# Layer four of a gated attention and mixture-of-experts network: two half blocks of the shared expert side by side, and one batch's routed results added by GpSimd

## What is computed

```python
# x: (4, 256, 256), normed row by row before it comes in; I_SH = 704, E = 8 experts, top 2, I_MOE = 176
probs = softmax(x @ W_router.T);  rw, sel = top_k(probs, 2)
g, u = split(x @ Ws_gate_up, 704)                    # shared expert, every token
sh = (silu(g) * u) @ Ws_down
shared_out = sh * sigmoid(x @ W_sgate.T)
gu = einsum('th,ehi->eti', x, We_gate_up)            # routed experts, two a token
eo = einsum('eti,eih->eth', silu(gu[..., :176]) * gu[..., 176:], We_down)
x_out = x + tanh(g_ffn[3]) * (shared_out + weighted sum of the token's two eo)
```

## Time and profile before

| | |
|---|---|
| median of 3 runs | 852.88 us (851.64, 852.88, 859.55) |
| profiled execution, its own time | 859.66 us |
| its span, first to last instruction | 857.9 us |
| busy: PE, DVE, ACT, POOL | 715.5, 546.8, 348.9, 206.9 us |
| mean granted TensorE clock | 0.908 |
| stage of the shared expert on PE | about 714 to 775 us |
| 23 routed tiles on PE | about 777 to 837 us |
| end: shared down 2 and 3, results back, stores | 837 to 858 us |

### The profile page before, as it was taken

The page is one execution under the profiler, slowest core; times in us unless marked ns, Lnnn a source line. Parts: engine busy times, 40 slices in busy tenths (PEclk is TensorE's granted clock), DMA queues, the critical chain, the costliest instruction groups (busy, mean ns, idle before and its releaser), DMA issues. The chain is left out here.

```text
span 857.9 us, 13857 instructions
## 1 busy us (share of the span) xinstructions
PE 715.5 (83%) x4399; PEld 473.9 (55%) x4399; DVE 546.8 (64%) x1655; ACT 348.9 (41%) x617; POOL 206.9 (24%) x299
## 2 busy tenths in 40 slices
PE   9999987878877745968786998976888889998995
PEld 4543556656764632646665776743233226776774
DVE  6787888886755965577675453445876856513554
ACT  2653555555437611512013413425468784212220
POOL 0003782001000220011413451542233220251331
PEclk9999999998888966879998799998589999999998
DMA  6993420400000400000133050012000033032314
GB/s 201 337 204 96 140 87 8 140 11 2 3 1 1 148 1 0 1 1 1 54 116 118 32 185 26 22 53 70 1 2 3 1 124 82 26 111 61 104 66 166
DMA packets 55487, 60.17 MB, mean 70 GB/s; under 512 B 13832, under 2 KB 48729, under 8 KB 55417
## 3 DMA queue, kind: packets, MB, share of 16 engines
q1 hardware_dynamic: 50328, 45.96, 18.8%
q0 software_dynamic: 4848, 13.28, 4.4%
q10 hardware_dynamic: 240, 0.05, 0.0%
HBM read 34.86 MB, written 24.20 MB: 69 GB/s over the span
## 5 line engine op out<-in xcount | busy, mean ns | idle before, releaser
L1856 ACT ACTIVATE arenas<-psum 128x512 f32<-128x512 f32 (+5 forms) x81 | 55.4, 703 | 59.7 <-PE psum L1095 40.5
L3053 DVE TENSOR_REDUCE arenas<-psum 128x2 f32<-128x512 f32 x96 | 62.1, 685 | 19.6 <-PE psum L1652 18.3
L1095 PE MATMUL psum<-conb,shared 128*128 128x128 bf16 (+2 forms) x512 | 41.7, 240 | 19.4 <-POOL shared L909 9.2
L907 POOL TENSOR_SCALAR arenas<-arenas,small 128x1024 f32<-128x1024 f32 x8 | 9.0, 1121 | 202.4 <-DVE small L2798 202.4
L1095 PEld LDWEIGHTS psum<-conb,shared 128*128 128x128 bf16 (+2 forms) x512 | 36.5, 126 | 27.6 <-issue 16.1
L921 POOL DMA_INDIRECT experts_l<-shared,small x30 | 29.2, 975 | 82.4 <-ACT shared L2148 70.5
L1543 PE MATMUL psum<-arenas,early 128*128 128x256 f32 (+1 forms) x192 | 43.9, 383 | 1.3 <-issue 1.0
L1856 ACT ACTIVATE late<-psum 128x512 f32<-128x512 f32 (+1 forms) x51 | 24.5, 504 | 48.2 <-PE psum L1095 48.1
L1095 PE MATMUL psum<-con,early 128*128 128x128 f32 (+1 forms) x188 | 32.5, 294 | 11.7 <-DVE early L2296 4.0
L2192 ACT ACTIVATE early<-psum 128x1024 f32<-128x1024 f32 x32 | 32.4, 1036 | 23.5 <-PE psum L1669 23.2
L3018 DVE TENSOR_TENSOR shared<-shared,psum 128x128 f32<-128x128 f32 x30 | 8.5, 286 | 51.3 <-PE psum L1605 29.2
(11 more groups left out here) (435 smaller groups left out, 1819.2 us busy)
## 6 DMA issues: line engine op xcount, KB each, us to landing
sorted_l<-late SPq DMA_DIRECT2D x3, 1920.0 KB, 17.8
early<-sorted_l SPq DMA_DIRECT2D x6, 645.0 KB, 5.8
early<-in_L_ffn_sw SPq DMA_DIRECT2D x3, 1024.0 KB, 9.0
late<-sorted_l SPq DMA_DIRECT2D x23, 129.0 KB, 2.0
sorted_l<-late SPq DMA_DIRECT2D x1, 2944.0 KB, 24.0
early<-in_L_ffn_We_gate_up SPq DMA_DIRECT2D x2, 1408.0 KB
early<-in_L_ffn_expert_w SPq DMA_DIRECT2D x2, 1024.0 KB, 6.9
early<-in_L_ffn_w SPq DMA_DIRECT2D x1, 2048.0 KB, 8.3
```

The source lines that it names most:

```text
L907: pool.tensor_scalar(ha[s][:, rows], ha[s][:, rows], c2[s][:, t:t + 1], ROUND, ALU.mult, ALU.add)
L1095: last = pe.transpose(v[0:parts, at:at + k], src, idn[0:k, 0:k])
L1856: act.activation(dst, view(v), ACT.Copy, scale=scale).then_inc(f.drained(i, key), 1)
L3053: dve.tensor_reduce(nm, q3d(f.slot(0, ("max", w, k)), 2, S), X, ALU.max, negate=True)\
```

## The change

It does two things in layer four's feed-forward.

First, the half blocks of a pair of batches (0 and 1, 2 and 3) share one bank. Batches 0 and 2 have five blocks. The sixth entry of batch 1 (and 3) holds 64 features of batch 0 in partitions 0 to 63 and the same 64 features of batch 1 in partitions 64 to 127; `blocks3(n)` gives the blocks of a batch. Gate and up of such an entry are eight matmuls with a weight of 64 columns each, in turn for the lower and the upper half. ACT and DVE treat the entry as a whole block. The down product takes the 64 features of its batch from the half where they lie, so the last 64 rows of Ws_down are loaded twice, once into each half (a fourth load under "l3s"). Since down 0 now needs the last entry of batch 1, and down 2 that of batch 3, their waits name it. Two of batch 2's blocks are put before down 0, and DVE's `add_shared(0, 0)` moves behind the second block of batch 2.

Second, POOL adds the routed results of batch 3 to x: four tensor_scalar with the weights, one tensor_tensor that sums the two experts, one tensor_tensor into x, then it signals x3_ready. DVE adds batches 0 to 2 as before, does `add_shared(1, 2)` ahead of them, and `add_shared(1, 3)` last, behind POOL's signal.

```diff
@@ plan of stage l3f
-             B=([0, 1, 2, 3], 1, [("sh", n, j) for n in range(B) for j in range(SC3)]))
+             B=([0, 1, 2, 3], 1, [("sh", n, j) for n in range(B) for j in blocks3(n)]))   # range(SC3 - 1 + n % 2)
@@ SP
-            load(q3d(ws_dn, SC3, D)[0:H_S3 - (SC3 - 1) * P, SC3 - 1], Ws_down[(SC3 - 1) * P:H_S3, :], "l3s")
+            for s in range(2):
+                load(q3d(ws_dn, SC3, D)[s * HALF_SH:(s + 1) * HALF_SH, SC3 - 1], Ws_down[(SC3 - 1) * P:H_S3, :], "l3s")
@@ POOL, at its end
+            n = B - 1
+            pool.wait_ge(back_in[n], 16)
+            for k in range(2):
+                for t in range(T):
+                    at = n * T + t
+                    pool.tensor_scalar(back[:, n, t, k], back[:, n, t, k], wsel[:, k, at:at + 1], None, ALU.mult)
+            pool.drain()
+            pool.tensor_tensor(back[:, n, :, 0], back[:, n, :, 0], back[:, n, :, 1], ALU.add)
+            pool.drain()
+            x = q3d(xs[:, n, :], T, D)
+            pool.tensor_tensor(x, x, back[:, n, :, 0], ALU.add)
+            pool.drain().then_inc(x3_ready.sem, 1)
@@ PE, shared3, the shared entry (j == SC3 - 1)
+                    for half in range(2):
+                        for c in range(DC):
+                            at = c * 2 * H_S3 + half * H_S3 + j * P
+                            for s in range(2):
+                                mm = pe.matmul(v[s * HALF_SH:(s + 1) * HALF_SH, half * S:(half + 1) * S], ws_gu[:, at:at + HALF_SH],
+                                               xnT3[n - 1 + s][:, c * S:(c + 1) * S], start=(c == 0), stop=(c == DC - 1))
@@ PE, shared_down3
-                pe.wait_ge(fb.drained(0, ("sh", n, SC3 - 1)), fb.read(0, ("sh", n, SC3 - 1)))
+                last = ("sh", n | 1, SC3 - 1)
+                pe.wait_ge(fb.drained(0, last), fb.read(0, last))
@@ PE, the stage
             rank(pl["l3k"]["A"], 0, 2 * B, picked)
+            shared3(2, blocks3(2)[0:2])
             shared_down3(0, 0)
-            shared3(0, 2)
+            shared3(2, blocks3(2)[2:])
             shared_down3(0, 1)
-            shared3(0, 3)
+            shared3(3, blocks3(3))
             routed3()
@@ DVE
-            add_shared(0, 0)
-            hidden3(0, 2, lambda j: None)
+            hidden3(0, 2, lambda j: add_shared(0, 0) if j == 1 else None)
...
+            add_shared(1, 2)
             for n in range(B):
-                if n >= 2:
+                if n == B - 1:
+                    dve.wait_ge(x3_ready.sem, x3_ready.count(ON_POOL))
                     add_shared(1, n)
-                add_routed(n)
+                else:
+                    add_routed(n)
                 dve.drain().then_inc(x_done.sem, 1)
```

More of the change, by code:

```diff
@@ L25 @@
 SC3 = -(-H_S3 // P)
+HALF_SH = H_S3 - (SC3 - 1) * P
+assert HALF_SH == P // 2
 HALF3 = H_R3 // 2
@@ L618, in flamingo_gated, with blocks3 @@
              V=([6, 7], 1, [(name, w) for w in range(UNITS) for name in ("pv", "tok")]))
+        def blocks3(n):
+            return range(SC3 - 1 + n % 2)
         plan("l3f", 0, A=([4, 5], 1, [(key, n) for p in range(2) for key in ("xT", "gate") for n in (2 * p, 2 * p + 1)]
                           + [("dn", 0), ("dn", 1)]),
-             B=([0, 1, 2, 3], 1, [("sh", n, j) for n in range(B) for j in range(SC3)]))
+             B=([0, 1, 2, 3], 1, [("sh", n, j) for n in range(B) for j in blocks3(n)]))
         plan("l3k", 0, A=([6], 1, [("rank",)]))
@@ L1754, in attention3, with shared3 @@
                 values3(UNITS - 1, 3)
-            def shared3(i, n):
-                for j in range(SC3):
-                    shared_up(pl["l3f"]["B"], i, n, j, xnT3, min(P, H_S3 - j * P), j * P, H_S3 + j * P, ws_gu, ws_gu, 2 * H_S3)
+            def shared3(n, blocks):
+                f = pl["l3f"]["B"]
+                for j in blocks:
+                    if j < SC3 - 1:
+                        shared_up(f, 0, n, j, xnT3, P, j * P, H_S3 + j * P, ws_gu, ws_gu, 2 * H_S3)
+                        continue
+                    pe.wait_ge(f.drained(0, ("sh", n, j)), f.empty(0, ("sh", n, j)))
+                    v = f.slot(0, ("sh", n, j))
+                    for half in range(2):
[4 more added lines that the diff above has]
+                                               xnT3[n - 1 + s][:, c * S:(c + 1) * S], start=(c == 0), stop=(c == DC - 1))
+                    mm.then_inc(f.filled, 1)
             def shared_down3(i, n):
@@ L1766, in shared_down3 @@
                     for j in range(SC3):
-                        r = min(P, H_S3 - j * P)
-                        mm = pe.matmul(v[:, t * D:(t + 1) * D], hsT3[n][0:r, j * S + t * P:j * S + (t + 1) * P],
-                                       ws_dn[0:r, j * D:(j + 1) * D], start=(j == 0), stop=(j == SC3 - 1))
+                        r, hs = slice(0, P), hsT3[n]
+                        if j == SC3 - 1:
+                            r, hs = slice(n % 2 * HALF_SH, (n % 2 + 1) * HALF_SH), hsT3[n | 1]
+                        mm = pe.matmul(v[:, t * D:(t + 1) * D], hs[r, j * S + t * P:j * S + (t + 1) * P],
+                                       ws_dn[r, j * D:(j + 1) * D], start=(j == 0), stop=(j == SC3 - 1))
                 mm.then_inc(fa.filled, 1)
@@ L1831, in _ @@
                 logits(pl["l3f"]["A"], 0, n, xnT3, r3T, E + 1)
-            pe.wait_ge(ld["l3s"], 16 * 3)
-            shared3(0, 0)
+            pe.wait_ge(ld["l3s"], 16 * 4)
+            shared3(0, blocks3(0))
             rows_turned3(1)
@@ L1836, in _ @@
                 logits(pl["l3f"]["A"], 0, n, xnT3, r3T, E + 1)
-            shared3(0, 1)
+            shared3(1, blocks3(1))
             banks_free("l3k", 0)
@@ L2218, in shared3 @@
                 gate = (ACT.Tanh, 0.5) if n == 0 else (ACT.Silu, 1.0)
-                for j in range(SC3):
+                for j in blocks3(n):
                     act.wait_ge(fb.filled, fb.full(i, ("sh", n, j)))
-                    v, r = fb.slot(i, ("sh", n, j)), min(P, H_S3 - j * P)
-                    act.activation(sg3[fb.place(i, ("sh", n, j))][0:r, :], v[0:r, 0:S], gate[0], scale=gate[1])\
+                    v = fb.slot(i, ("sh", n, j))
+                    act.activation(sg3[fb.place(i, ("sh", n, j))], v[:, 0:S], gate[0], scale=gate[1])\
                        .then_inc(sg3_ready, 1)
@@ L3175, in hidden3 @@
                 fb = pl["l3f"]["B"]
-                for j in range(SC3):
+                for j in blocks3(n):
                     dve.wait_ge(fb.filled, fb.full(i, ("sh", n, j)))
-                    r, v = min(P, H_S3 - j * P), fb.slot(i, ("sh", n, j))
-                    sg = sg3[fb.place(i, ("sh", n, j))][0:r, :]
+                    v, sg = fb.slot(i, ("sh", n, j)), sg3[fb.place(i, ("sh", n, j))]
                     dve.wait_ge(sg3_ready, fb.full(i, ("sh", n, j)))
-                    gated(sg, v[0:r, 0:S], n == 0)
-                    dve.scalar_tensor_tensor(hsT3[n][0:r, j * S:(j + 1) * S], v[0:r, S:2 * S], 0.5 if n == 0 else 1.0, sg,
+                    gated(sg, v[:, 0:S], n == 0)
+                    dve.scalar_tensor_tensor(hsT3[n][:, j * S:(j + 1) * S], v[:, S:2 * S], 0.5 if n == 0 else 1.0, sg,
                                              ALU.mult, ALU.mult).then_inc(fb.drained(i, ("sh", n, j)), 1)
```

## The result

The changed kernel is slower: 857.6 us median of 14 runs (852.35 to 863.4) against 855.32 us of 14 runs of the kernel before, taken beside it (851.64 to 864.32). The ratio is 1.0048, with a 95% interval of 1.0026 to 1.0071, so 2.2 to 6.1 us slower. The ratio is taken over the fast runs and is not the quotient of the two medians, which is 1.0027 and lies at the lower end of that interval. I had forecast 1.6 us faster. The profiled execution took 862.8 us; its span is 861.0.

What follows compares the result with a forecast made beforehand. PE was taken to bound the shared stage and routed tiles, DMA then DVE the last 20 us. Terms -3.9 (stage) + 2.3 (tail) = -1.6 us, so 852.88 - 1.6 = 851.3 us, range 846.5 to 855.5.

Steps and rivals of the forecast that it cites:

- The first term: Shared expert's stage on PE: with shared entries the first routed transpose comes 3.9 us earlier.
- the second, the tail: End of the kernel: with POOL adding batch 3's routed results, batch 3 is done 2.3 us later.
- The nearest row: Attention's four matmuls in four column groups, 1.00 us together; from it a shared entry on PE was priced at 1.87 us.
- what its 3.9 had over 3.7: PE's stage: entries save 3.7 us; the rest of 3.9 was put down to the 0.17 us wait at 722.00 going.
- Rival 1: PE's shared entries: column groups do not overlap, an entry costs 3.6 us, total 854.9 us; chance 0.08.
- the rule on weight loads: PE's shared entries: a weight load overlaps a running matmul only where row groups differ; spoke partly for no overlap.
- rival 3: PE's 2 us stall around 766 is bound to POOL's sends and may vanish or double: 849.3 or 853.3; chance 0.15.
- I take 0.55: POOL's tail: each of four tensor_scalar of 128x256 takes 0.55 us, 2.2 together, between a cast's 0.400 and 0.765.
- Drains and signals some 0.2: POOL's tail: drains and signals take some 0.2 us of the 4.8 us chain after batch 3 lands.
- my upper end of 3.1: POOL's tail: upper end for the four tensor_scalar together, 3.1 us, with 2.2 expected and 1.6 the lower end.
- rival 2: Tail: batch 3's results are back earlier, at 849.3, so the tail costs nothing, total 849.0; chance 0.2.
- the 0.5 that I had put beside the sum: Tail: DVE's addition of batch 2 might delay POOL's start by up to 0.5 us; left out of the sum.

Runs made afterwards that it cites:

- e10_order_alone: Kernel before with only DVE's shared additions of batches 2 and 3 moved among its routed ones, at waits; ratio to before 1.0018 (0.9993 to 1.0042).
- e2_pool: Kernel before with only the change's second part, POOL adding batch 3's routed results; ratio to before 1.0081 (1.0048 to 1.0114).
- e9_halves_in_turn: e1_entry with each shared entry's matmuls ordered two lower, then two upper, in each of gate and up; one run, end 15.89 us.
- e1_entry: Changed kernel without POOL's additions and with DVE's end as before; 850.73 against 854.81 us, ratio to before 0.9968 (0.9936 to 1.0001).
- e5_drain: Changed kernel with one POOL drain added behind the loop that writes expert results; one run, end 19.60 us.
- e7_drain_two_ops: Changed kernel with both mends: a POOL drain behind the expert-result writes, a second operation (times 1.0) on the four tensor_scalar; 850.49 against 855.79 us, ratio 0.9946.
- e6_drain_mid: Changed kernel with one POOL drain added between its 16 sends of sorted rows and 23 writes of expert results; one run, end 20.70 us.
- e4_warm: Changed kernel with a tiny POOL tensor_tensor and a drain added ahead of its wait for batch 3; ratio to before 1.0001 (0.9973 to 1.0029).

## Why the prediction was wrong

The sum was -3.9 + 2.3 = -1.6 us. The first term was right and the second, the tail, was mis-sized.

**The shared entries.** The nearest row, four column groups side by side, told the price of an entry to 0.01 us: 1.88 measured, 1.87 predicted. Without disturbance the distance to the first routed transpose is 60.65 us (e10_order_alone) and 56.4 us with the entries (after and four experiments): 4.2 us gained, 3.9 predicted. Two disturbed profiles give the same 60.7 once their disturbance is taken off: before without its stall of 1.7 us, e2_pool without 1.7 us at a lower clock. The prediction put what its 3.9 had over 3.7 down to the wait of 0.17 us at 722.00; that wait is still there (0.16 us at 726.60). Of the 4.2, what the entries do not explain is 0.2 us less of waiting in front of the first transpose (1.81 instead of 2.00 in e10_order_alone), 0.2 in the two down products and 0.1 in batch 0. PE had no wait of note before the rank, and the gathered rows were there, as predicted. Rival 1 fell. This case's traces do not bear out the rule on weight loads that spoke for it (TensorE: Matmul & The Clock Gate, The mechanism, in the Trainium skill): all eight matmuls of an entry use all rows and take 1.88 us, and in e9_halves_in_turn, with neighbours of one group, 1.93.

In the two profiles that I compared the gain was 6.0 us, for before held the stall around 766 us (12.48 us for six blocks, where e10_order_alone takes 10.77). That was rival 3, and it did fall away; but it is not bound to POOL's sends, since e2_pool has the same sends and does not have it there. What I wrote ahead of the sum, that both stages lie at full clock and hold nothing special in that execution, was wrong. Other executions show another disturbance of this size: PE's granted clock. In e1_entry, by stretches of 2 us (the seventh column is the clock):

```profile
724.00:726.00 2.00, 1.66 (x16) 1.45 (x14) 1.64 (x6) 0.94 (x2) 0.00 (x0) 1.00 0.00 0
726.00:728.00 2.00, 2.00 (x10) 1.71 (x10) 1.77 (x10) 0.00 (x0) 0.00 (x0) 0.69 0.00 0
728.00:730.00 2.00, 2.00 (x6) 1.56 (x5) 0.87 (x8) 0.85 (x6) 0.00 (x0) 0.50 0.00 0
730.00:732.00 2.00, 2.00 (x10) 1.79 (x9) 0.00 (x0) 1.97 (x7) 0.00 (x0) 0.96 0.00 0
```

Five whole blocks took 10.57 us there and 8.88 in after: 1.7 us. The same 10.57 stand in e5_drain and e7_drain_two_ops. And before the routed tiles, where PE waits some 2 us, in before:

```profile
776.00:778.00 2.00, 0.58 (x4) 0.40 (x4) 0.22 (x2) 0.39 (x1) 0.00 (x0) 1.00 0.00 0
778.00:780.00 2.00, 2.00 (x6) 1.19 (x6) 0.00 (x0) 0.38 (x1) 0.00 (x0) 0.55 0.48 127
780.00:782.00 2.00, 2.00 (x7) 1.29 (x6) 0.56 (x2) 0.70 (x2) 0.00 (x0) 0.59 0.05 13
```

and after:

```profile
776.00:778.00 2.00, 1.64 (x8) 1.04 (x8) 0.00 (x0) 0.77 (x2) 0.00 (x0) 1.00 0.30 82
778.00:780.00 2.00, 1.78 (x10) 1.06 (x8) 0.56 (x3) 0.98 (x3) 0.00 (x0) 1.00 0.20 58
```

0.5 is the lower of PE's two levels, 1.2 GHz. It costs 1.2 us of the 23 tiles (60.2 us in before against 59.1 in after, and 59.2 in e10_order_alone, whose code is the same there as that of before). These come and go between executions of like code; what decides them is not settled here.

**The tail.** The step that failed is the price of POOL's chain: "It has four tensor_scalar of 128x256 ... I take 0.55", "Drains and signals some 0.2. POOL is done at 851.7 + 4.8". It put 4.8 us where 9.8 were measured. From the landing of batch 3 to POOL's signal it took 9.8 us, from 847.6 to 857.4. Against the sum: the tensor_scalar 3.70 instead of 2.2 us, beyond even my upper end of 3.1; the drain 3.35 us, in neither end and 3.2 of it the price of the 39 indirect transfers before it; the two tensor_tensor 2.5 instead of 2.4. The landing itself came 1.6 us sooner than I reckoned from before (7.0 us after its issue instead of 8.6), a part of rival 2. 1.5 + 3.35 + 0.15 - 1.6 = 3.4 us, and the end grew by 5.7 instead of 2.3. Of the 6.3 us between the forecast of 851.3 and the 857.6 measured, 2.4 are none of these: the kernel before measured 855.32 us over 14 runs and 852.88 over the three that I started from.

Both were to be seen. In the earlier trace rows I read the durations of the rows and not their last column. The 1.4 us of idle time in front of L950 are the price of the drain behind 15 indirect transfers (shown at e6_drain_mid), and I put drains at 0.2 us. The 7.2 us in front of L853 are something else: that operation follows eight indirect transfers with no drain between, and no run here says what POOL does then. And I took the nearest row by shape and not by form: both rows used for the price were of other forms (a cast, and a tensor_scalar with two operations), while the kernel has tensor_scalar with one operation and a weight from a tensor, of 128x32, at 0.37 us:

```profile
L1011 POOL TENSOR_SCALAR early<-early,small 128x32 f32<-128x32 f32 x3 | 1.1, 373 | 2.7 <-DVE early L3121 2.7
```

Little of that is a start-up cost: from this row to the 0.91 us at 256 columns the form costs (0.91 - 0.37) / 224 = 2.4 ns a column, while the form with two operations took 0.765 us for 512 columns, 1.5 ns a column with everything in it.

**The Trainium skill's lock.** SBUF — State Buffer, Who interferes with whom, would have POOL and DVE exclude each other while DVE adds batch 2. The trace agrees in part, by single operations. DVE's last operation on batch 2 in after took 0.70 us instead of 0.48 (so its four took 2.06 instead of 1.84), and POOL's first, under way at the same time, 0.99 instead of 0.91. In e5_drain POOL's first took 1.23 and DVE's stayed at 0.48; in e4_warm, the most disturbed, POOL's first two took 1.07 and 1.18 and the four 4.05 instead of 3.70. On POOL's chain it is worth 0.1 to 0.4 us, below the 0.5 that I had put beside the sum; in after it was 0.1.

**What stays open.** The undisturbed distances add up to -4.2 + 5.7 = +1.5 us for the change, and 4.1 us (2.2 to 6.1) were measured. The 5.7 is itself from one profile each: ends with POOL's part as in the change are 21.68 and 21.95 us, ends with DVE's old order 15.65 to 16.42, so it may be 5.3 to 6.3 and the sum +1.1 to +2.1. Each part alone leans the same way: e1_entry -2.7 us (-5.5 to +0.1) where its distances say -4.1, e2_pool +6.9 (4.1 to 9.7) where they say +5.4. The medians lie nearer in two of the three: +2.3 us for the change, -4.1 for e1_entry and +7.9 for e2_pool. One profile of each kernel cannot say whether the end is longer in other executions, or whether something upstream is. That the result lies within 1%, for which I had put 0.91, says nothing for the mechanism.

## What to carry to other kernels

Before work is moved to an idle engine, add its chain in series from the moment its input is there, and price each operation from a row of the same form, with the same kinds of scalars. On GpSimd, look at the idle time under "issue" as a price too, and count the indirect transfers since the last drain: put a drain behind the last of them, where the engine would wait anyway, and do not leave it to the first drain on the path. Before giving work away, see whether the engine that has it stands idle at a wait: here two lines moved on DVE gave 0.3 to 1.3 us of the end, though no gain in time that the runs can tell, and the move to POOL lost 1.5 us of the end even with both mends.

## What the runs showed of the hardware

- A drain on GpSimd took 0.15 us and 0.082 us more for each indirect transfer (of 128 rows) issued since the last drain: 3.35 us for 39 in after, 2.04 for 23 in e6_drain_mid, 1.39 for 15 and 0.49 for 4 in before. It did so even when all had landed. Two drains begun within 2 us of the last write took 0.7 and 1.2 us more than that.
- On GpSimd a tensor_scalar of 128x256 float32 with a scalar from a tensor took 0.91 us with one operation and 0.47 us with a second one (times 1.0) added, where DVE was not at work beside it; the means of four were 0.93 and 0.52.
- DVE's scalar_tensor_tensor with its inputs in SBUF took 0.70 instead of 0.48 us beside GpSimd's first tensor_scalar in after, and that one 0.99 instead of 0.91.
- Two column groups of 64 ran fully beside each other: eight float32 matmuls of 128*64 by 256 took 1.88 us, four took 1.87, and 1.93 us in the other order.
- TensorE's granted clock fell to 0.5 for some 3 us inside dense work in e1_entry, behind short matmuls and a wait of 0.34 us, and did not in after at the same place of the program. It cost 1.7 us there.
